# A new order of the four engines' calls in the first stage, and a chain of waits between the last 16 scatters

## Chip, cores and metric

The kernel runs on one core of one Trainium2 chip. The metric is the device time of one execution in microseconds (us), lower being better; a comparison goes by the median of several runs.

## The reference

Input `x` has 16 sequences of 256 tokens with 128 channels, 4096 tokens in all, in float32. Two blocks follow each other, each with a residual and a plain layer norm behind it. The first is an RWKV block: layer norms, a shift by one token, three 128x128 projections (key, value, receptance), a recurrence over time, an output projection, and then a channel mix with a hidden width of 512. The second is a mixture of experts with 12 experts, top 2, beside a shared expert.

```python
x = L0_attn_x
x = layernorm(x + attn(x))          # ln0, ln1, shift, k/v/r, wkv, Wo, ln2, channel mix
def ffn(x):
    ys = geglu(xf @ Ws1 + bs1) @ Ws2 + bs2            # shared expert, hidden 256
    logits = (xf @ Wr + br) / 1.5
    top_val, top_idx = top_k(logits, 2); w = softmax(top_val)
    yE[e] = geglu(xf @ We1[e] + be1[e]) @ We2[e] + be2[e]   # hidden 384
    return ys + sum_k w_k * yE[top_idx_k]
x = layernorm(x + ffn(x))
```

## The kernel before

**Two stages.** The 4096 tokens are 32 tiles of 128, and 4 tiles make a chunk of 512, so there are 8 chunks (0 to 7). The first stage takes every chunk through the RWKV block, the router and the shared expert. The second stage takes 75 tiles of 128 rows, sorted by expert, through their expert, and a last part adds everything up and norms it.

**Four engines, four lists written out by hand.** In the first stage each step is a small function that one engine calls with a chunk number, and every engine runs its own list of calls, strictly in that order: DVE at L690 to L709, ACT at L839 to L864, POOL at L943 to L956, PE at L1140 to L1162. Steps wait for one another through semaphores inside the functions. The order of a list decides what an engine does while something it will need later is not ready yet; a wait at the head of a list holds up all that is behind it.

**The steps that matter here.** DVE: `stats0` to `stats3` (L482 to L526, the statistics of the norms), `prepare` (L442, mixes the weights that `keys(0)` needs), `maximum`, `gaps`, `weigh_v`, `states`, `carried`, `one_over`, `output` (the recurrence), `mix`, `x3` (L596, end of the block's two residuals), `logits`, `chosen` (L337) and `placed` (L361, the row number to which each token's copy goes), `shared_act` (L622) and `shared_take` (L630), `find_tiles` and `tell_tiles` (L642, L672, the list of tiles, in two parts). ACT: `norm0` to `norm3`, `affine1`, `below`, `factors`, `by_channel` (L777), `shared_gelu` (L824), `place_pad` (L829, one small DMA each), `first_take`. POOL: `deviation` (L891, 1/sqrt of the variance), `weigh0`, `shift0`, `add_new`, `residual` and `scatter_rows` (L405). PE: `turn1` to `turn3` (transposes, L965 to L968), `keys`, `values`, `receptance`, `rwkv`, `hidden`, `mixed_channels` (L1055), `router` (L1026), `prefix`, `shared_gate` (L1094), `shared_up` (L1088), `shared_back` (L1100), `tell` (L1111), `first_turn`, `first_gates`.

**The scatters.** Each of the 32 tiles is written twice, once for each chosen expert, by an indirect DMA issued on POOL's queue (L413): 128 rows of 544 bytes go to places in DRAM by the indices of `placed`. That is 64 scatters. `placed(v, b)` frees 16 of them at a time (`slots_ready`). The first 48 count on the semaphore `dispatched`, the last 16 (`LATE` = 48) on `dispatched_late`. POOL does not wait for their landing.

**Who reads the scattered rows.** SP waits until the first 48 have landed and then loads rows for tiles 0 to 4 and onward (L1189), ten buffers deep. The first 35 tiles (`AHEAD`) need the first 48 scatters alone; only ahead of tile 35 does SP wait for the late 16. Behind its last scatter POOL's queue goes on with the second stage, where it issues one indirect DMA for each finished tile (L1235, 128 rows of 512 bytes to `routed_rows`) when DVE has written `yo` (L1288). There are ten `yo` buffers (`YO` = 10), so DVE waits ahead of tile n for the landing of tile n-10.

**The second stage's start.** PE needs both parts of the tile list (`bias_ready` at 2), seven of the eight `shared_take`, all `shared_gelu`, and the first rows and weights. Its last work of the first stage is `shared_up(7, 1)` and `shared_back(7)`; `tell(1)`, nine small products, makes the second part of the tile list.

## Time and profile before

| | us |
|---|---|
| median of 3 runs (461.55 to 463.85) | 462.53 |
| the profiled execution | 463.21 |
| its span in the profile | 461.4 |
| PE / DVE / ACT / POOL busy | 390.9 / 310.2 / 293.0 / 246.7 |

Times inside the profile count from the start of the span; some 1.8 us of the execution's own time lie around the span. PE is TensorE, PEld its weight loads, DVE VectorE, ACT ScalarE, POOL GpSimd, SP the queue that issues the plain DMAs. The first stage ends where the first matmul of L1396 starts. In the chain of work that ended last, "another core or an unknown queue" (also "remote") stands where a wait ended on a semaphore whose last update the profile cannot lay to an instruction that ended just then. There is one core here, so it is no other core: it is a signal that came long after the record of the instruction that gives it.

### The profile page before, as it was taken

The page shows a single profiled execution, that of the slowest core. Times are in us where ns is not written, and L with a number is a line of the kernel's source. Part 1 is how long each engine was busy: PE and PEld are TensorE (multiplying, and loading weights), DVE is VectorE, ACT ScalarE, POOL GpSimd, SP SyncE. Part 2 cuts the span into 40 slices and gives each one's busy share as a digit, 9 for nine tenths or more (in the row PEclk, how much of TensorE's full clock was granted, in tenths as well). Part 3 has the DMA queues.
Part 4 walks back from the last instruction along what each step waited for, and adds up shares of the span by engine and source line. Part 5 has one row for each costly group of instructions (what it writes and reads, how often), then busy time and mean ns, then how long its engine had stood idle before and what let it go on. Part 6 is the DMA issues. An engine that isn't in the chain of part 4 may idle for free.

```text
span 461.4 us, 9878 instructions
## 1 busy us (share of the span) xinstructions
PE 390.9 (85%) x2487; PEld 302.6 (66%) x2487; DVE 310.2 (67%) x1097; ACT 293.0 (64%) x723; POOL 246.7 (53%) x300
## 2 busy tenths in 40 slices
PE   0757799998988888976799499999999999999690
PEld 0224466757746565654344179999999999999530
DVE  6979988999996995741372266666666656665183
ACT  4478799989796955633121067777777766777062
POOL 4756855648388867777347114444444444444252
PEclk9978799999999999997899599999999999999997
DMA  8699100000003101011262137777776776762483
GB/s 230 151 288 348 46 0 1 1 1 1 2 18 104 32 13 44 30 50 42 82 203 83 54 136 248 259 244 261 247 254 243 258 250 238 253 239 104 132 328 106
DMA packets 47248, 64.86 MB, mean 141 GB/s; under 512 B 8797, under 2 KB 31069, under 8 KB 47193
## 3 DMA queue, kind: packets, MB, share of 16 engines
q1 hardware_dynamic: 42584, 54.50, 34.9%
q0 software_dynamic: 4448, 9.38, 6.1%
q8 instruction: 22, 0.36, 0.4%
q10 hardware_dynamic: 160, 0.35, 0.3%
q14 instruction: 34, 0.27, 0.2%
HBM read 21.65 MB, written 13.91 MB: 77 GB/s over the span
## 4 chain that ended last, share of the span: by engine, by line
PE 55%; DVE 14%; ACT 9%; another core or an unknown queue 8%; issue 5%; POOL 4%; DMA 2%; POOLq 0%; SPq 0%; DVEq 0%; ACTq 0%
PE bank L1396 22%; PE bank L1414 11%; DVE bst L487 3%; PE bank L1042 3%; ACT z L725 2%; PE bank L1060 2%; PE bank L1441 2%; PE bank L1108 2%; PE bank L1388 2%; DVE rec L576 1%; PE bank L1091 1%; DMA we_sb<-routed_rows 1%; PE bank L983 1%; PE bank L1071 1%
## 5 line engine op out<-in xcount | busy, mean ns | idle before, releaser
L1235 POOL DMA_INDIRECT routed_rows<-yo,goes_to x75 | 71.8, 957 | 103.8 <-DVE yo L1288 101.4
L1396 PE MATMUL bank<-xT,w 128*128 128x128 f32 x896 | 112.9, 275 | 0.0
L1396 PEld LDWEIGHTS bank<-xT,w 128*128 128x128 f32 x896 | 106.4, 192 | 0.8 <-issue 0.5
L1280 DVE SCALAR_TENSOR_TENSOR actT<-bank,tile_bias,gl 128x128 f32<-128x128 f32 x225 | 65.4, 346 | 24.8 <-ACT gl L1348 13.5
L413 POOL DMA_INDIRECT dispatched_rows<-rows_all,slot_i x64 | 64.3, 1005 | 30.1 <-issue 17.7
L1348 ACT ACTIVATE gl<-bank,tile_bias 128x128 f32<-128x128 f32 x225 | 66.2, 363 | 15.2 <-PE bank L1396 7.9
L1414 PE MATMUL bank<-we_sb,actT 128*128 x450 | 62.8, 276 | 1.0 <-DVE yo L1288 0.9
L1414 PEld LDWEIGHTS bank<-we_sb,actT 128*128 128x128 f32 x450 | 56.1, 192 | 1.5 <-issue 1.5
L1288 DVE SCALAR_TENSOR_TENSOR yo<-bank,goes,wb 128x128 f32<-128x128 f32 x75 | 26.3, 351 | 36.7 <-PE bank L1414 33.0
L1342 ACT ACTIVATE xT<-bank 128x128 f32<-128x128 f32 x74 | 20.5, 277 | 25.2 <-PE bank L1388 24.9
L1042 PE MATMUL bank<-xk,wfk_sb 128*128 128x512 f32 x64 | 33.0, 625 | 3.4 <-DVE xk L593 1.8
L1358 ACT ACTIVATE wb<-be_all,goes 128x128 f32 x75 | 30.1, 402 | 6.2 <-issue 5.5
L627 DVE SCALAR_TENSOR_TENSOR below_m<-bank,v_sb,below_p 128x512 f32<-128x512 f32 x16 | 11.8, 749 | 32.1 <-remote 24.4
L1060 PEld LDWEIGHTS bank<-wfv_sb,kf 128*128 128x128 f32 x256 | 29.4, 192 | 5.1 <-ACT kf L822 4.6
L983 PE MATMUL bank<-hT,mixa 128*128 128x512 f32 x48 | 27.0, 646 | 6.6 <-ACT hT L761 5.7
L1060 PE MATMUL bank<-wfv_sb,kf 128*128 128x128 f32 x256 | 30.4, 277 | 2.3 <-ACT kf L822 2.3
L827 ACT ACTIVATE below_p<-bank,v_sb 128x512 f32<-128x512 f32 x16 | 10.9, 684 | 31.1 <-PE bank L1097 17.8
L576 DVE RECIPROCAL rec<-nd 128x512 f32<-128x512 f32 x8 | 26.7, 3341 | 0.0
L984 PE MATMUL bank<-hT,mixb 128*128 128x512 f32 x48 | 26.0, 625 | 0.0
L1091 PE MATMUL bank<-xnT_all,ws_sb 128*128 128x512 f32 x32 | 18.9, 683 | 6.0 <-DVE below_m L627 6.0
L818 ACT ACTIVATE kf<-bank 128x512 f32<-128x512 f32 x32 | 18.6, 588 | 6.0 <-PE bank L1042 4.3
L1378 ACT ACTIVATE x_all<-bank,fnm,frs 128x128 f32<-128x128 f32 x28 | 10.5, 456 | 15.9 <-POOL fnm L1244 15.9
(220 smaller groups left out, 764.6 us busy)
## 6 DMA issues: line engine op xcount, KB each, us to landing
w<-we_sb SPq DMA_DIRECT2D x75, 384.0 KB
x_all<-dispatched_rows SPq DMA_DIRECT2D x75, 68.0 KB
we_sb<-we SPq DMA_DIRECT2D x1, 4608.0 KB
we_sb<-routed_rows SPq DMA_DIRECT2D x8, 512.0 KB, 7.4
rows_all<-x SPq DMA_DIRECT2D x8, 256.0 KB, 5.1
out<-x_all SPq DMA_DIRECT2D x8, 256.0 KB, 2.3
routed_rows<-yo,goes_to POOLq DMA_INDIRECT x75
dispatched_rows<-rows_all,slot_i POOLq DMA_INDIRECT x64
```

Of the source, the lines that this page charges most:

```text
L413: ng.indirect_dma_start(dispatch, bass.IndirectOffsetOnAxis(ap=slot_i[:, k, n:n + 1], axis=0), rows_all[:, n, :], None).then_inc(s["dispat ...
L576: nv.reciprocal(rec[:, :], nd[:, 1, :]).then_inc(s["rec_ready"], 1)
L983: nt.matmul(o, mixa[:, n, :], hT[:, :, 1:T + 1], start=True, stop=False)
L1042: nt.matmul(pf[j % 2][:, :], wfk_sb[:, j * P:(j + 1) * P], xk2[:, :], start=True, stop=True).then_inc(s["fk_ready"], 1)
L1060: last = nt.matmul(pkv[:, n * P:(n + 1) * P], kf[:, j, n * P:(n + 1) * P], wfv_sb[:, j, :], start=j == 0, stop=j == HF - 1)
L1235: ng.indirect_dma_start(routed, bass.IndirectOffsetOnAxis(ap=goes_to[n // U % DB][:, n % U:n % U + 1], axis=0), yo[n % YO][:, :], None).th ...
L1280: nv.scalar_tensor_tensor(actT[n % UA][:, at], ps_a[j][:, 0:P], tile_bias[:, j, n:n + 1], gl[n % 2][:, at], ALU.add, ALU.mult).then_inc(s2 ...
L1288: nv.scalar_tensor_tensor(yo[n % YO][:, :], ps_y[:, 0:C], goes[n // U % DB][:, n % U, 1:2], wb[n % 2][:, :], ALU.mult, ALU.add).then_inc(s ...
L1348: na.activation(gl[n % 2][:, j * P:(j + 1) * P], ps_g[j][:, 0:P], ACT.Gelu, bias=tile_bias[:, HK + j, n:n + 1]).then_inc(s2["gelu_ready"], 1)
L1358: na.activation(wb[n % 2][:, :], be2_all[:, ds(e * C, C)], ACT.Copy, scale=goes[n // U % DB][:, n % U, 1:2]).then_inc(s2["wb_ready"], 1)
L1396: return nt.matmul(to[:, 0:P], w1[m][:, off:off + P], xT[m][:, :], start=True, stop=True)
L1414: last = nt.matmul(ps_y[:, 0:C], actT[m][:, j * P:(j + 1) * P], we2_sb[:, ds(e, 1), j, :].rearrange("p a c -> p (a c)"), start=j == 0, sto ...
```

## The change

Two things. In `scatter_rows` each of the last 16 scatters but the first waits until the one ahead of it has landed (16 increments of `dispatched_late` for each). And the four lists of the first stage stand in another order. No step is added or left out, and every step is the same as before; the second stage is not touched. In the cut diff a line of "..." stands for lines of the lists that are left out.

```diff
@@ -410,6 +410,8 @@
                 for b, (lo, hi) in enumerate(BATCH):
                     if n == lo * CT and k == 0:
                         g.wait_ge(s["slots_ready"], b + 1)
+                if i > LATE:
+                    g.wait_ge(s["dispatched_late"], 16 * (i - LATE))
                 ng.indirect_dma_start(dispatch, bass.IndirectOffsetOnAxis(ap=slot_i[:, k, n:n + 1], axis=0), rows_all[:, n, :],
                                       None).then_inc(s["dispatched_late" if i >= LATE else "dispatched"], 16)
 
@@ -687,26 +689,27 @@
-            stats0(0); turn_rows(); stats0(1); first_rows(); stats1(0); prepare(); stats0(2); stats0(3); number_rows(); stats0(4); stats1(1); stats0(5); maximum(0); gaps(0)
-            stats0(6); stats1(2); weigh_v(0); states(0); carried(0); maximum(1); gaps(1); one_over(0); output(0)
...
-            stats2(7); chosen(v, 2); shared_act(0, 1); x3(6); mix(7); stats3(6)
-            shared_act(1, 0); placed(v, 2, pT[:, PT_PREFIX]); find_tiles(0); leave_tiles(); x3(7); shared_act(1, 1); stats3(7)
-            shared_take(0); logits(6); shared_act(2, 0); shared_act(2, 1); tell_tiles(0); logits(7); chosen(v, 3)
-            shared_take(1); shared_act(3, 0); shared_act(3, 1); placed(v, 3, pT[:, PT_PREFIX])
-            count_pads(); shared_act(4, 0); shared_act(4, 1); shared_take(2); shared_take(3); find_tiles(1); shared_act(5, 0)
-            shared_act(5, 1); shared_take(4); shared_act(6, 0); shared_act(6, 1); shared_take(5); tell_tiles(1)
-            shared_act(7, 0); shared_act(7, 1); shared_take(6); shared_take(7)
+            stats0(0); turn_rows(); stats0(1); first_rows(); stats1(0); stats0(2); stats0(3); prepare()
+            stats0(4); stats1(1); stats0(5); maximum(0); gaps(0); number_rows(); stats0(6); stats0(7); stats1(2)
...
+            stats2(7); placed(v, 1, pT[:, PT_PREFIX]); shared_act(1, 0); logits(5); chosen(v, 2); mix(7)
+            shared_take(0); shared_act(1, 1); x3(6); stats3(6); placed(v, 2, pT[:, PT_PREFIX]); find_tiles(0)
+            x3(7); stats3(7); shared_act(2, 0); shared_take(1); shared_act(2, 1); logits(6); shared_act(3, 0)
+            shared_act(3, 1); leave_tiles(); tell_tiles(0); logits(7); chosen(v, 3); shared_take(2)
+            shared_act(4, 0); shared_act(4, 1); placed(v, 3, pT[:, PT_PREFIX]); count_pads(); shared_take(3)
+            shared_take(4); shared_act(5, 0); shared_act(5, 1); find_tiles(1); shared_act(6, 0)
+            shared_act(6, 1); shared_take(5); shared_act(7, 0); shared_act(7, 1); tell_tiles(1); shared_take(6)
+            shared_take(7)
...
@@ -836,32 +839,32 @@
-            norm0(0); decays(); norm0(1); norm1(0); affine1(0); norm0(2); norm1(1); below(0); factors(0); gate(0)
-            affine1(1); norm0(3); norm1(2); below(1); factors(1); norm0(4); affine1(2); gate(1); x1(0); norm1(3)
...
-            relu(7, 1); square(7, 1); relu(7, 2); square(7, 2); relu(7, 3); square(7, 3); norm3(6)
-            shared_gelu(1, 1); gate2(7); by_channel(6); shared_gelu(2, 0); shared_gelu(2, 1)
-            norm3(7); by_channel(7); shared_gelu(3, 0); shared_gelu(3, 1); fallen(a, 3)
-            shared_gelu(4, 0); shared_gelu(4, 1); place_pad(7); shared_gelu(5, 0); place_pad(8)
-            shared_gelu(5, 1); place_pad(9); shared_gelu(6, 0); place_pad(10); shared_gelu(6, 1); place_pad(11)
-            shared_gelu(7, 0); first_take(0); shared_gelu(7, 1)
+            norm0(0); norm0(1); norm1(0); decays(); affine1(0); norm0(2); norm0(3); norm1(1); below(0)
+            factors(0); affine1(1); norm1(2); norm0(4); gate(0); below(1); norm0(5); factors(1); x1(0); gate(1)
...
+            square(7, 3); norm3(6); shared_gelu(2, 0); gate2(7); shared_gelu(2, 1); shared_gelu(3, 0); norm3(7)
+            by_channel(6); shared_gelu(3, 1); by_channel(7); shared_gelu(4, 0); fallen(a, 3); shared_gelu(4, 1)
+            shared_gelu(5, 0); shared_gelu(5, 1); shared_gelu(6, 0); place_pad(7); shared_gelu(6, 1)
+            place_pad(8); place_pad(9); shared_gelu(7, 0); shared_gelu(7, 1); place_pad(10); place_pad(11)
+            first_take(0)
...
@@ -940,20 +943,17 @@
-            deviation0(0); deviation0(1); deviation(0, "1"); weigh0(1)
-            shift0(1); deviation0(2); deviation(1, "1"); weigh0(2); shift0(2)
-            deviation(2, "1"); deviation0(3); add_new(0); weigh0(3); shift0(3); weigh0(4); deviation(3, "1")
-            deviation(0, "2"); add_new(1); deviation0(4); shift0(4); residual(0); weigh0(5)
-            deviation(4, "1"); deviation(1, "2"); shift0(5); add_new(2); deviation(0, "3"); residual(1)
-            deviation(5, "1"); deviation(2, "2"); add_new(3); residual(2); deviation(1, "3")
-            weigh0(6); shift0(6); deviation(3, "2"); add_new(4); weigh0(7); deviation(6, "1")
-            shift0(7); deviation(2, "3"); deviation(7, "1"); residual(3); deviation(4, "2"); add_new(5)
-            residual(4); deviation(3, "3"); scatter_rows(g, 0, 7); deviation(5, "2"); scatter_rows(g, 7, 9)
-            add_new(6); scatter_rows(g, 9, 11); deviation(4, "3"); scatter_rows(g, 11, 13); residual(5)
-            scatter_rows(g, 13, 15); deviation(6, "2"); scatter_rows(g, 15, 16); add_new(7); deviation(5, "3")
-            residual(6); scatter_rows(g, 16, 23); deviation(7, "2"); scatter_rows(g, 23, 28); residual(7)
-            scatter_rows(g, 28, 29); deviation(6, "3"); scatter_rows(g, 29, 38); deviation(7, "3")
-            scatter_rows(g, 38, SLOTS // P)
+            deviation0(0); deviation0(1); deviation(0, "1"); deviation0(2); weigh0(1); shift0(1); weigh0(2)
+            deviation(1, "1"); shift0(2); deviation0(3); weigh0(3); shift0(3); deviation0(4); deviation(2, "1")
+            add_new(0); weigh0(4); shift0(4); weigh0(5); shift0(5); deviation(3, "1"); deviation(0, "2")
+            add_new(1); deviation(4, "1"); weigh0(6); residual(0); add_new(2); deviation(1, "2"); residual(1)
+            deviation(0, "3"); shift0(6); deviation(5, "1"); deviation(2, "2"); add_new(3); weigh0(7); shift0(7)
+            residual(2); deviation(1, "3"); deviation(3, "2"); deviation(6, "1"); add_new(4); residual(3)
+            deviation(2, "3"); deviation(7, "1"); deviation(4, "2"); add_new(5); residual(4); deviation(3, "3")
+            deviation(5, "2"); add_new(6); scatter_rows(g, 0, 7); residual(5); deviation(4, "3")
+            scatter_rows(g, 7, 9); add_new(7); deviation(6, "2"); scatter_rows(g, 9, 16); residual(6)
+            deviation(5, "3"); deviation(7, "2"); scatter_rows(g, 16, 23); residual(7); deviation(6, "3")
+            scatter_rows(g, 23, 29); deviation(7, "3"); scatter_rows(g, 29, SLOTS // P)
...
@@ -1137,29 +1137,30 @@
-            turn1(0); keys(0); values(0); receptance(0); turn1(1); keys(1); turn1(2); receptance(1); values(1)
-            rwkv(0); values(2); keys(2); turn2(0); receptance2(0); hidden(0, 0); turn1(3); receptance(2)
...
-            shared_up(1, 1); turn3(6); shared_gate(2, 0); router(6); shared_gate(2, 1); shared_up(2, 0); tell(0)
-            shared_gate(3, 0); shared_back(1); turn3(7); shared_up(2, 1); router(7); shared_up(3, 0)
-            shared_gate(3, 1); shared_back(2); shared_up(3, 1); prefix(3); shared_gate(4, 0); shared_back(3)
-            shared_up(4, 0); shared_gate(4, 1); shared_up(4, 1); shared_gate(5, 0); shared_back(4)
-            shared_gate(5, 1); shared_up(5, 0); shared_up(5, 1); shared_gate(6, 0); shared_gate(6, 1)
-            shared_back(5); shared_up(6, 0); shared_gate(7, 0); shared_up(6, 1); tell(1); shared_gate(7, 1)
-            shared_up(7, 0); shared_back(6); first_turn(0); shared_up(7, 1); first_turn(1); first_gates(); shared_back(7)
+            turn1(0); keys(0); values(0); turn1(1); receptance(0); keys(1); receptance(1); values(1); rwkv(0)
+            turn1(2); keys(2); turn2(0); values(2); receptance2(0); turn1(3); hidden(0, 0); hidden(0, 1)
...
+            hidden(7, 3); prefix(2); receptance2(7); mixed_channels(7); shared_back(1); shared_gate(2, 1)
+            shared_gate(3, 0); shared_up(2, 1); shared_up(3, 0); turn3(6); shared_back(2); shared_up(3, 1)
+            shared_gate(3, 1); router(6); tell(0); turn3(7); shared_gate(4, 0); router(7); shared_back(3)
+            shared_gate(4, 1); shared_gate(5, 0); shared_up(4, 0); shared_up(4, 1); prefix(3); shared_up(5, 0)
+            shared_back(4); shared_gate(5, 1); shared_up(5, 1); shared_gate(6, 0); shared_up(6, 0)
+            shared_up(6, 1); shared_gate(6, 1); shared_back(5); shared_gate(7, 0); shared_gate(7, 1)
+            shared_back(6); shared_up(7, 0); shared_up(7, 1); tell(1); first_turn(0); shared_back(7)
+            first_turn(1); first_gates()
```

In the part of the lists that is cut out the calls are shifted against one another by a few places: on DVE `number_rows`, `stats0(7)` and the later `stats1` calls, on PE `rwkv` earlier against `hidden`, on ACT `norm0` and `norm1` earlier against `relu` and `square`.

## Rows read from the trace of the kernel before

**Rows 1.** The page: chain of work that ended last, by engine

```profile
PE 55%; DVE 14%; ACT 9%; another core or an unknown queue 8%; issue 5%; POOL 4%; DMA 2%; POOLq 0%; SPq 0%; DVEq 0%; ACTq 0%
```

**Rows 2.** The chain in order of time, 200 to 260: start, us, what

```profile
200.83 10.34 another core or an unknown queue
...
217.94 7.77 another core or an unknown queue
...
246.67 12.49 another core or an unknown queue
```

**Rows 3.** Timeline of PE, 203 to 269: start, us, engine, line, operation [idle before]

```profile
203.25 0.60 PE L967 MATMUL bank<-ident,rows_all 128*128 128x128 f32 x4
...
248.50 1.02 PE L1091 MATMUL bank<-xnT_all,ws_sb 128*128 128x512 f32 x2
...
251.64 1.51 PE L1121 MATMUL bank<-of_expert,be_sb 12*128 12x40 f32 x12
253.07 1.12 PE L1097 MATMUL bank<-xnT_all,ws_sb 128*128 128x512 f32 x2
260.18 2.04 PE L1091 MATMUL bank<-xnT_all,ws_sb 128*128 128x512 f32 x2 [5.98 <-DVE below_m L627]
262.01 3.20 PE L1108 MATMUL bank<-below_m,ws_sb 128*128 128x512 f32 x4
...
267.12 1.98 PE L1108 MATMUL bank<-below_m,ws_sb 128*128 128x512 f32 x4
268.95 1.05 PE L1396 MATMUL bank<-xT,w 128*128 128x128 f32 x8
```

**Rows 4.** Timelines of ACT and DVE: what ended the two longest of those waits

```profile
211.19 0.60 ACT L779 ACTIVATE xnT_all<-bank 128x512 f32<-128x512 f32 x1 [10.36 <-remote]
```

```profile
259.28 1.41 DVE L627 SCALAR_TENSOR_TENSOR below_m<-bank,v_sb,below_p 128x512 f32<-128x512 f32 x2 [12.61 <-remote]
```

**Rows 5.** Timeline of POOL: scatters 29, 38, 47, 48, 63, then the second stage's

```profile
198.26 1.03 POOL L413 DMA_INDIRECT dispatched_rows<-rows_all,slot_i  x1 [0.16 <-issue]
...
211.33 1.03 POOL L413 DMA_INDIRECT dispatched_rows<-rows_all,slot_i  x1 [0.16 <-issue]
...
222.77 0.96 POOL L413 DMA_INDIRECT dispatched_rows<-rows_all,slot_i  x1 [0.31 <-issue]
236.08 0.96 POOL L413 DMA_INDIRECT dispatched_rows<-rows_all,slot_i  x1 [12.36 <-DVE slot_i L383]
...
255.01 0.95 POOL L413 DMA_INDIRECT dispatched_rows<-rows_all,slot_i  x1 [0.31 <-issue]
273.55 0.96 POOL L1235 DMA_INDIRECT routed_rows<-yo,goes_to  x1 [17.59 <-DVE yo L1288]
275.67 0.96 POOL L1235 DMA_INDIRECT routed_rows<-yo,goes_to  x1 [1.16 <-DVE yo L1288]
```

**Rows 6.** Busy time by stretch: start:end, length, PE, PEld, DVE, ACT, POOL, PEclk, DMA, GB/s

```profile
60.00:200.00 140.00, 128.74 (x736) 89.57 (x735) 120.33 (x344) 115.94 (x224) 93.56 (x115) 1.00 0.07 22
...
204.70:211.90 7.20, 0.01 (x1) 0.00 (x1) 3.84 (x13) 0.60 (x1) 5.94 (x9) 0.87 0.14 48
...
246.70:259.20 12.50, 7.50 (x31) 3.79 (x29) 0.00 (x0) 0.80 (x2) 7.13 (x8) 0.81 0.21 67
259.20:269.00 9.80, 8.67 (x19) 3.92 (x20) 5.46 (x14) 2.44 (x6) 0.00 (x0) 0.72 0.16 43
269.00:300.00 31.00, 31.00 (x275) 30.65 (x274) 19.77 (x73) 22.12 (x73) 12.44 (x13) 1.00 0.67 235
```

**Rows 7.** The chain at the end: the last tile's indirect DMA, issue to landing

```profile
430.62 2.50 DMA routed_rows<-yo,goes_to
```

**Rows 8.** Timelines of DVE and PE at the start

```profile
14.18 0.87 DVE L487 BATCH_NORM_STATS2 bst<-rows_all 128x6 f32<-128x128 f32 x4
...
16.55 0.16 DVE L468 CAST x_all<-pad_i 128x23 f32<-128x23 int32 x1
```

```profile
15.56 2.07 PE L983 MATMUL bank<-hT,mixa 128*128 128x512 f32 x2 [0.66 <-ACT hT L755]
```

More of the change, by code:

```diff
@@ new lines, in attention_scalar @@
+            affine2k(1); norm0(7); gate2(1); x1(2); norm3(0); relu(1, 0); square(1, 0); gate(3); by_channel(0)
+            relu(1, 1); relu(1, 2); affine1(4); square(1, 1); square(1, 2); norm2(2); relu(1, 3); square(1, 3)
+            norm1(5); affine2(2); affine2k(2); below(4); factors(4); gate2(2); x1(3); norm3(1); gate(4)
+            affine1(5); relu(2, 0); relu(2, 1); norm2(3); relu(2, 2); relu(2, 3); by_channel(1); square(2, 3)
+            square(2, 1); square(2, 0); square(2, 2); norm1(6); affine2k(3); affine2(3); below(5); factors(5)
@@ new lines, in attention_scalar @@
+            relu(3, 0); x1(4); square(3, 0); relu(3, 1); gate2(3); norm3(2); relu(3, 2); affine1(6)
+            square(3, 2); relu(3, 3); norm2(4); by_channel(2); square(3, 1); square(3, 3); norm1(7)
+            fallen(a, 0); affine2k(4); affine2(4); gate(5); below(6); gate2(4); factors(6); x1(5); norm3(3)
+            relu(4, 0); by_channel(3); relu(4, 1); gate(6); affine1(7); norm2(5); relu(4, 2); relu(4, 3)
+            square(4, 2); square(4, 0); square(4, 1); square(4, 3); affine2(5); below(7); factors(7)
@@ new lines, in attention_tensor @@
+            turn2(3); values(5); mixed_channels(2); router(1); rwkv(4); hidden(3, 0); hidden(3, 1)
+            receptance2(3); turn1(6); hidden(3, 2); receptance(5); hidden(3, 3); turn3(2); keys(6); values(6)
+            turn2(4); mixed_channels(3); receptance2(4); rwkv(5); router(2); receptance(6); hidden(4, 0)
+            hidden(4, 1); turn3(3); hidden(4, 2); turn1(7); hidden(4, 3); prefix(0); keys(7); turn2(5)
+            values(7); mixed_channels(4); receptance2(5); rwkv(6); shared_gate(0, 0); router(3); hidden(5, 0)
@@ new lines, in attention_tensor @@
+            hidden(5, 1); shared_up(0, 0); hidden(5, 2); hidden(5, 3); shared_gate(0, 1); shared_up(0, 1)
+            turn3(4); receptance(7); mixed_channels(5); turn2(6); rwkv(7); receptance2(6); router(4)
+            hidden(6, 0); hidden(6, 1); shared_gate(1, 0); hidden(6, 2); prefix(1); shared_back(0); hidden(6, 3)
+            turn3(5); shared_up(1, 0); shared_gate(1, 1); router(5); shared_up(1, 1); turn2(7)
+            shared_gate(2, 0); mixed_channels(6); hidden(7, 0); hidden(7, 1); shared_up(2, 0); hidden(7, 2)
```

67 lines of the change are left out of this document (24 added, 43 removed).

## The prediction

> **What bounds the kernel now.** I read the chain of work that ended last first. PE has 55% of it, and 8% stands as "another core or an unknown queue" [rows 1]. On one core that can only be a signal that came late. In order of time, three pieces make 30.6 us of it: 10.3, 7.8 and 12.5 us, all between 200 and 260 [rows 2]. So the end of the first stage, not its middle, holds the largest loss that is nobody's work.
>
> Next I asked what the late signals have in common. PE's four transposes of chunk 6 are recorded at 203.25 and take 0.6 us, yet ACT, which waits for them, starts at 211.19 [rows 3, 4]. The `shared_up(6, 0)` of 248.50 is done at 249.5, and the DVE instruction that reads it starts at 259.28 [rows 3, 4]. In both cases the signal that is late is PE's. PE then has nothing to do: 0.01 us busy of 7.2 in the stretch from 204.7 [rows 6]. POOL's timeline fits: these stretches are the ones in which POOL issues scatters back to back. Scatters 29 to 47 run from 198.26 to 222.77, with one norm step among them ahead of 38, and 48 to 63 from 236.08 to 255.01, one each 1.26 us (18.93 / 15) [rows 5]. Between the two bursts no such piece stands in the chain. The waits end soon after a burst does: 225.7 against the last issue at 222.77, 259.2 against 255.01 [rows 2, 5]. An indirect DMA on this queue needs 2.50 us from issue to landing [rows 7], so at a spacing of 1.26 two are always in flight. In the second stage they come 2.12 us apart [rows 5], and there PE is busy 31.0 of 31.0 us [rows 6]. My reading: scatters closer together than they land hold up PE's signals. It is an inference from when things happen; no row shows the path.
>
> From 60 to 200 the stage is another thing: PE is busy 128.7 of 140 us and DVE 120.3 [rows 6]. An order can win there only what PE idles, 11.3 us.
>
> **The change, part by part.** The sum goes against the profiled execution, 463.2 us (span 461.4 and 1.8 around it), which lies 0.7 above the median of 462.5.
>
> *The waits between the late scatters.* Each now costs POOL the landing, 2.50 us [rows 7], and the 0.3 us of issue that stands between two scatters already [rows 5]. The spacing grows from 1.26 to 2.8. From the first late scatter at 236.1 the last is issued at 236.1 + 15 x 2.8 = 278.1 instead of 255.0, and POOL is free at 279.1. Behind the waiting scatters on POOL's queue stands only the second stage: its first indirect DMA, now at 273.55 [rows 5]. SP needs the late rows ahead of tile 35, some 50 us after the second stage starts even with ten buffers of lead, so that wait hides. The direct cost is zero as long as ten `yo` buffers cover the delay: if the second stage starts 8 us earlier (below), the first `yo` is there at 265.3, and (279.1 - 265.3) / 2.12 = 6.5 tiles queue up, under ten. Without that cover, each tile over ten would cost 2.1 us.
>
> *What the waits free.* If one scatter in flight leaves PE's signals alone, the 12.5 us go. PE ran ahead in part: 7.5 us of work in the 12.5 [rows 6], up to 254.2 (253.07 + 1.12). From there it would go on at once. What it still did in the trace, from 260.18 to 268.95, is 8.77 us. Two pieces of it ran at the lower of the two clocks after PE's idle time: 2.04 against 1.02 for L1091 and 3.20 against 1.98 for L1108 [rows 3]; the granted clock of the stretch is 0.72, a mix of 2.4 and 1.2 GHz [rows 6]. Without the idle time these 2.2 us go too. So L1396 starts at 254.2 + 6.5 = 260.7 in place of 268.95: -8.2. The new list sets `tell(1)` behind `shared_up(7, 1)`; its twelve small products take 1.5 us [rows 3], and DVE's copies that all of the second stage waits for then run beside `shared_back(7)`. That is the same PE work at a worse place; I take 0.2 of loss, at most 1. Term: **-8**, bounds 0 (nothing is freed) and -12.5.
>
> *Scatters 29 to 47 behind the norm of chunk 7.* In the trace nine of them precede that norm's 1/sqrt; scatter 38 behind it starts at 211.33 [rows 5]. In the new list all 19 are behind it. So chunk 7's last norm, transpose and router should pass before the burst, where now ACT waits for chunk 6's transpose until 211.19 and for chunk 7's until 225.7 [rows 2, 4]. ACT's list also takes `norm3(7)` ahead of `by_channel(6)`, and PE gets five more shared products ahead of `turn3(6)`. Against that the burst starts later: at some 209 I would say, so its last scatter is issued at 209 + 18 x 1.26 = 231.7, 9 us later than 222.77, without a pause. The router's work no longer sits in it, but the shared expert's does, and the late 16 follow soon. SP's tile loads need the landing, 234.2; they then take a few us and the second stage needs them only at 260. Bounds: -11 (the 10.3 and most of what PE loses with it go) and +8.5 (the same stall, ending that much later). PE does some work even in a stall (7.5 of 12.5 [rows 6]), so I stay near the middle: **-2**.
>
> *The start.* `prepare()` moves behind `stats0(2)` and `stats0(3)`, which take 14.18 to 16.55 [rows 8]. The mixed weights, ready just ahead of 14.18, are then ready 2.4 later, at 16.5, and `keys(0)`, which starts at 15.56, starts 1 us later. In return the norm of chunks 2 and 3, and so `x0` of chunk 1, come up to 3 us earlier, and `number_rows` (1.2 us) leaves DVE's way to `maximum(0)`. **-1**, bounds -2 and +1.
>
> *The middle.* `rwkv`, `norm0`, `norm1`, `add_new` and the statistics shift by a few places. POOL now does `deviation(5, "2")` and `add_new(6)`, for which others wait, ahead of its first scatter; no step is added. With PE 92% busy I take **0**, bounds -4 and +5 (a misplaced call holds the recurrence of one chunk).
>
> Sum: 463.2 - 8 - 2 - 1 = **452.2**, say 452.
>
> **A rule against it.** The rows above tie PE's late signals to DMAs. The Trainium skill, "SBUF — State Buffer", section "SBUF: two separate sides", says that "A DMA cannot be slowed by a compute op, and vice versa". By that rule the scatters are innocent, the waits free nothing, and only the order works. This is the first rival below.
>
> **The rivals.**
>
> *The stall stays.* The late signals come from something else in these stretches (SP's pads and ACT's pads are issued there too), or four in a row suffice with any spacing. For it: the trace has stretches with scatters and no late signal, such as 236 to 246. Against it: all three long pieces lie in or just behind a burst. Then 463.2 - 1 - 2 = 460.2, with the new place of the burst uncertain; say 460.5.
>
> *The stall moves into the second stage: slower.* When POOL comes free at 279.1 it has 6.5 tiles to catch up, at 1.26 us each against 2.12 a tile: 13.8 / 0.86 = 16 indirect DMAs back to back. That is the same burst as the 16 late scatters, which cost 12.5 us, now in a stage where PE has no idle time at all [rows 6]. Price up to 12.5: 452.2 + 12.5 = 464.7, and about 465 to 469 when the first burst also ends later. It decides from a backlog of some three tiles on (seven in a row), that is, from a late chain that ends 6 us behind the first `yo`. For it: the arithmetic. Against it: these rows are 512 bytes, not 544, and the signals there have a tile of slack only in part.
>
> *Both stalls go.* Chunk 7 passes before the burst and the shared work no longer waits for PE's signals: -11 in place of -2, which gives 443 to 444.
>
> **How the numbers follow.** Forecast 0.52, stall stays 0.17, moved into the second stage 0.17, both go 0.14. A run of this kernel tells 0.5%, 2.3 us, from no change. Faster by more than that (under 460.2): the forecast and the last rival, less a little, with a few hundredths of the first, 0.67. Within: most of the first, 0.16. Slower: 0.17. The range takes in the last rival at its low end and the first at its high end: 444 to 462; only the slower rival and some tail are left out.
>
> **What would show it.** Right: late scatters 2.5 to 3 us apart; no "unknown" piece of over 3 us while they run; PE at its upper clock in the last 10 us of the first stage; L1396 first at 255 to 260; POOL's first L1235 some 13 us behind its `yo`. Wrong: the piece of 12 us still there with the late scatters 2.8 apart (the rule above holds); PE with idle time between 275 and 300 (moved); a piece of over 15 us at 210 to 235 (the burst). If the stage reaches 200 more than 3 us off, the middle was mispriced.

## The result, and the profile after

The changed kernel took **473.7 us** (472.8 to 474.7, 4 runs) beside 463.2 us for the kernel before on the same chip (461.6 to 464.1, 4 runs): ratio 1.0246, 95% interval 1.0204 to 1.0288. Forecast were 452 and a range of 444 to 462. The change is slower, and the forecast had the wrong sign.

| | before | after |
|---|---|---|
| profiled execution, span | 463.2, 461.4 | 472.8, 471.0 |
| first gate products of the experts (L1396, now L1397) | 268.95 | 259.92 |
| from there to the end | 192.5 | 211.1 |
| first / last late scatter | 236.08 / 255.01 | 240.16 / 285.22 |
| POOL's first indirect DMA of the second stage | 273.55 | 286.48 |

So the first stage is 9.0 us shorter, where 11 were forecast, and the second 18.6 longer, where 0 was forecast. The page of after, part 4 (the chain that ended last, by engine), against [rows 1]:

```profile
PE 47%; DVE 12%; DMA 11%; POOL 8%; issue 8%; ACT 6%; another core or an unknown queue 5%; POOLq 0%; DVEq 0%; ACTq 0%; SPq 0%
```

DMA has 11% of the chain where it had 2%; 9% are landings of POOL's scatters, by the same part of the page. The unknown part fell from 8% to 5% only. The chain's longest pieces from 200 us on say where (start, us, what), against [rows 2]:

```profile
212.95 6.01 another core or an unknown queue
220.49 12.12 another core or an unknown queue
...
258.55 2.26 DMA dispatched_rows<-rows_all,slot_i
261.08 3.39 DMA dispatched_rows<-rows_all,slot_i
264.74 4.11 DMA dispatched_rows<-rows_all,slot_i
269.12 3.30 DMA dispatched_rows<-rows_all,slot_i
...
282.05 2.91 DMA dispatched_rows<-rows_all,slot_i
285.22 0.96 POOL dispatched_rows L415
```

Two things are to be seen. The 18.1 us in the first burst (two pieces) are as long as before (10.3 and 7.8), and the piece of 12.5 us ahead of the second stage is gone. But the late chain, which the waits turn into landing after landing, runs on until POOL starts on the second stage's DMAs. Its landings take 2.3 to 2.5 us until 260; behind that, with SP loading a tile every 2.12 us beside them, they take 2.3 to 4.1. What follows, on DVE and PE, against [rows 5, 6]; first the timeline of DVE (start, us, engine, line, operation, count, idle time before and who ended it):

```profile
289.31 0.35 DVE L1289 SCALAR_TENSOR_TENSOR yo<-bank,goes,wb 128x128 f32<-128x128 f32 x1 [5.04 <-DMA routed_rows<-yo,goes_to]
289.58 0.86 DVE L1281 SCALAR_TENSOR_TENSOR actT<-bank,tile_bias,gl 128x128 f32<-128x128 f32 x3
...
297.27 0.35 DVE L1281 SCALAR_TENSOR_TENSOR actT<-bank,tile_bias,gl 128x128 f32<-128x128 f32 x1 [4.96 <-remote]
```

Then PE's:

```profile
290.11 1.65 PE L1415 MATMUL bank<-we_sb,actT 128*128 x6 [4.07 <-DVE yo L1289]
...
295.56 0.49 PE L1397 MATMUL bank<-xT,w 128*128 128x128 f32 x2 [0.46 <-ACT gl L1349]
297.67 0.49 PE L1397 MATMUL bank<-xT,w 128*128 128x128 f32 x2 [1.62 <-issue]
299.80 0.54 PE L1397 MATMUL bank<-xT,w 128*128 128x128 f32 x2 [1.64 <-DVE actT L1281]
```

And busy time by stretch (stretch, length, then busy us of PE, PEld, DVE, ACT, POOL; granted clock; DMA share; GB/s):

```profile
60.00:200.00 140.00, 134.27 (x769) 93.44 (x769) 120.94 (x341) 115.85 (x223) 86.41 (x107) 1.00 0.06 20
...
280.00:290.00 10.00, 6.04 (x55) 5.80 (x53) 3.41 (x14) 4.60 (x16) 4.79 (x5) 0.99 0.66 228
290.00:300.00 10.00, 6.17 (x34) 5.61 (x35) 1.56 (x6) 1.48 (x4) 7.59 (x8) 0.84 0.17 54
300.00:320.00 20.00, 16.89 (x118) 16.19 (x118) 9.26 (x34) 11.02 (x35) 7.14 (x9) 0.74 0.48 167
```

This is one chain of events with two losses. All ten `yo` buffers are full, so DVE waits 5.04 us for the first landing (its releaser is the DMA). Then POOL sends twelve DMAs 1.26 us apart (286.48 to 300.37), and in that burst PE gets on by two products every 2.1 us, where the twelve of a tile otherwise take 1.5; DVE's wait of 4.96 us ends by a signal of PE's that is late (`remote`). The clock falls to a mix of its two levels (0.74 from 300 to 320) and the pace of 2.12 us a tile is back only at 311. The sign that the prediction had named for a moved stall, PE with idle time between 275 and 300, is there: 12.2 us busy of the 20 from 280 on.

### The profile page after: what moved, and what is told of

Read it like the earlier page. It is cut to its first block, busy times and chain, and to the rows that moved or that the text cites. A ratio compares the mean times of both kernels' runs of the same rounds, so it can differ in the third digit from the quotient of the medians.

```text
span 471.0 us, 9878 instructions
## 1 busy us (share of the span) xinstructions
PE 395.1 (84%) x2487; PEld 305.5 (65%) x2487; DVE 309.7 (66%) x1097; ACT 292.2 (62%) x723; POOL 245.8 (52%) x300
## 4 chain that ended last, share of the span: by engine, by line
PE 47%; DVE 12%; DMA 11%; POOL 8%; issue 8%; ACT 6%; another core or an unknown queue 5%; POOLq 0%; DVEq 0%; ACTq 0%; SPq 0%
PE bank L1397 19%; PE bank L1415 10%; DMA dispatched_rows<-rows_all,slot_i 9%; PE bank L1442 3%; PE bank L1060 3%; PE bank L1042 2%; ACT z L728 2%; PE bank L983 2%; PE bank L984 2%; DVE rec L578 1%; DVE bst L489 1%; PE bank L1389 1%; POOL rstd L915 1%; POOL rstd L903 1%
## 5 line engine op out<-in xcount | busy, mean ns | idle before, releaser
L1397 PE MATMUL bank<-xT,w 128*128 128x128 f32 x896 | 116.3, 280 | 5.8 <-DVE actT L1281 3.2
L1397 PEld LDWEIGHTS bank<-xT,w 128*128 128x128 f32 x896 | 109.1, 196 | 6.9 <-DVE actT L1281 3.7
L415 POOL DMA_INDIRECT dispatched_rows<-rows_all,slot_i x64 | 62.9, 982 | 56.3 <-DMA dispatched_rows<-rows_all,slot_i 30.7
L1415 PE MATMUL bank<-we_sb,actT 128*128 x450 | 65.0, 282 | 6.6 <-DVE yo L1289 5.0
L1415 PEld LDWEIGHTS bank<-we_sb,actT 128*128 128x128 f32 x450 | 58.0, 197 | 7.6 <-issue 7.6
L983 PE MATMUL bank<-hT,mixa 128*128 128x512 f32 x48 | 28.5, 678 | 11.0 <-ACT th L810 5.7
L1042 PE MATMUL bank<-xk,wfk_sb 128*128 128x512 f32 x64 | 32.0, 605 | 2.3 <-ACT kf L821 2.3
L984 PE MATMUL bank<-hT,mixb 128*128 128x512 f32 x48 | 27.2, 651 | 0.0
L830 ACT ACTIVATE below_p<-bank,v_sb 128x512 f32<-128x512 f32 x16 | 10.8, 682 | 22.8 <-PE bank L1097 16.1
L944 POOL TENSOR_TENSOR s<-x1c,rows_all 128x512 f32<-128x512 f32 x8 | 10.5, 1318 | 27.4 <-DVE x3c L607 27.0
L983 PEld LDWEIGHTS bank<-hT,mixa 128*128 128x128 f32 x48 | 8.8, 213 | 20.6 <-issue 12.2
```

The source lines that it names most:

```text
L415: ng.indirect_dma_start(dispatch, bass.IndirectOffsetOnAxis(ap=slot_i[:, k, n:n + 1], axis=0), rows_all[:, n, :], None).then_inc(s["dispat ...
L983: nt.matmul(o, mixa[:, n, :], hT[:, :, 1:T + 1], start=True, stop=False)
L984: nt.matmul(o, mixb[:, n, :], hT[:, :, 0:T], start=False, stop=True).then_inc(s[name], 1)
L1042: nt.matmul(pf[j % 2][:, :], wfk_sb[:, j * P:(j + 1) * P], xk2[:, :], start=True, stop=True).then_inc(s["fk_ready"], 1)
L1397: return nt.matmul(to[:, 0:P], w1[m][:, off:off + P], xT[m][:, :], start=True, stop=True)
L1415: last = nt.matmul(ps_y[:, 0:C], actT[m][:, j * P:(j + 1) * P], we2_sb[:, ds(e, 1), j, :].rearrange("p a c -> p (a c)"), start=j == 0, sto ...
```

## The experiments

Every experiment was timed beside the kernel before, in the same session on the same chip. One thing has to be told first, as it orders all that follows: **the sessions were of two kinds**. In three of them, that of the result among them, the kernel before took 463.0 to 463.8 us. In four it took 438.3 to 440.4, on four chips, and one of these was met in both kinds. I call the first kind sessions with late signals, and each trace shows by itself which kind it is from: in the eleven traces from sessions without them no wait at all is put down to `remote`, in the nine others 7 to 17 waits are, the longest of them 5.6 to 19.3 us. Otherwise the traces of one program differ little: that of the kernel before stays within 2.3 us of its counterpart (the kernel with a held DMA, further down, which is the same up to there) until 185 us and starts the second stage 22.7 behind it.

| | sessions without late signals | with |
|---|---|---|
| the kernel before | 438.3 to 440.4 us | 463.0 to 463.8 us |
| new order alone | 0.983, 0.982, 0.986 | 1.015, 1.019 (each with one more small edit) |
| waits alone, old order | 1.001 | 1.011 |
| **both: the change** | **1.013, 1.012** | **1.025** |
| waits in pairs | 0.983 | |
| the change with 14 `yo` buffers | | 1.016 |
| new order, nine more scatters ahead of chunk 7's norm | | 1.017 |
| the kernel before with a held DMA | 1.000 | |
| paced, scatter 48 on (1.8 us apart) | | 0.995 |
| paced, scatter 29 on (1.8 us), pads spread, 14 buffers | 1.003 | 0.972 |
| the same with 1.38 us for 29 to 47 | 0.986, 0.989 | |

(Ratios to the kernel before of the same session, as they are on record; the intervals are in the text, 0.003 to 0.008 to either side. A ratio need not be the quotient of the two medians beside it. For two kernels it matters: with 14 buffers the medians give 1.024, with nine scatters ahead 1.009. The kernel before took 455.4 to 465.3 us in that session.)

**The order alone** (session without late signals).

```diff
-                if i > LATE:
-                    g.wait_ge(s["dispatched_late"], 16 * (i - LATE))
```

> The changed kernel without the waits: the new order alone. Theory A (the order is worth little, the waits win in the first stage and lose more in the second): the 16 late scatters run 1.26 us apart from about 240 to 259, a piece of about 12 us stands there again, L1395 (gate products of the experts) starts at 266 to 270 where it starts at 259.9 with the waits, POOL never queues more than one tile in the second stage, which then takes 192 us as before. Time 459 to 464. Rival B (the order is what costs): 470 or more, with the first burst of scatters, 29 to 47, as the place. Rival C (the second stage is slow for something else than the late chain, such as the weights' or rows' loads): second stage of over 200 us without the waits too, 469 or more.

432.4 us beside 439.2, ratio 0.983 [0.979, 0.986]: a gain that no theory had. Scatters 29 to 63 run in one burst of 35 (200.8 to 243.9, 1.27 apart), and the piece of 12 us that theory A expects of it is not there: no part of the chain is unknown. L1395 starts at 235.5.

```profile
PE 62%; DVE 11%; POOL 9%; issue 6%; ACT 6%; DMA 2%; POOLq 0%; DVEq 0%; ACTq 0%; SPq 0%
```

So here a burst held up nothing, and the order's own worth can be read. Busy time of PE, the kernel before (with its held DMA of tile 30, further down) and then the new order:

```profile
60.00:200.00 140.00, 129.70 (x736) 0.99 0.07 22
```

```profile
60.00:200.00 140.00, 136.66 (x776) 1.00 0.06 21
```

PE gets 7.0 us more done in the middle, for which I had taken 0. By 246.3 and 235.5 for the first gate products the whole first stage gives 10.8 (9.4 and 7.3 in the two repeats further down); the time falls by 5.3 to 8.5 us in the three.

**The waits alone** (same session), and later in one with late signals.

```diff
+                if i > LATE:
+                    g.wait_ge(s["dispatched_late"], 16 * (i - LATE))
```

> The kernel before with the waits alone, in the old order. Theory A: L1398 or so starts 6 to 9 us earlier than the 268.95 of before, the late chain lasts 45 us from 236 to 281, POOL is 6 to 8 tiles behind when it starts on the second stage's DMAs and sends 12 to 16 of them back to back; PE stalls there. With less backlog than in the changed kernel (its chain starts 4 us earlier) the loss is 10 to 18: 464 to 473. Rival B (the order is what costs): the waits alone give the 8 us and lose nothing, 453 to 457. Rival C: second stage 192 us whatever the late chain does.

439.7 beside 439.2, ratio 1.001 [0.998, 1.004]: nothing gained, nothing lost. Gate products from 245.2, POOL free at 265.5, first `yo` at 249.2: 7.7 tiles of backlog, under ten. The 19 DMAs back to back that follow cost nothing here.

> The kernel before with the waits alone once more, for the case that this is a chip with late signals (before at 463; then all of this holds): second stage begins 6 to 9 us earlier than 268.95, the late chain ends at about 281, some 7 tiles of backlog, 14 to 18 DMAs back to back in the second stage and a stall of 8 to 14 there: 463 to 470, ratio 1.00 to 1.015. Beside a kernel before of 439 it repeats 1.001.

467.2 beside 463.8, ratio 1.011 [1.004, 1.017]. Gate products from 260.7, which is 8.2 us ahead of the 268.95 of [rows 3], and the second stage takes 206.0. The backlog was 7.4 tiles (280.4 less 264.7, by 2.12), no buffer was short, and still 13 us went. DVE's longest wait in the burst and the chain:

```profile
287.38 0.35 DVE L1290 SCALAR_TENSOR_TENSOR yo<-bank,goes,wb 128x128 f32<-128x128 f32 x1 [5.78 <-remote]
```

```profile
282.33 7.77 issue
290.12 2.76 another core or an unknown queue
293.33 2.79 PE bank L1398 x10
```

The catch-up burst runs from 280.4 on. That is the burst's stall by itself, without the wait for a buffer.

**A burst put into the kernel before** (session without).

```diff
-                g.wait_ge(s2["yo_ready"], n + 1)
+                g.wait_ge(s2["yo_ready"], n + 1 if n != 30 else n + 8)
```

> The kernel before, with one edit in the second stage alone: POOL's DMA of tile 30 waits until DVE has given tile 37, so that eight are queued and then go back to back, as after the late chain, but with no scatter of the first stage, no full set of the ten buffers and 50 us later. Theory A (DMAs back to back hold up PE's signals, wherever they are): some 18 in a row at 1.26 us, PE in stalls of 5 to 12 us with the lower clock after it: 470 to 476. Rival C (the second stage's loss comes from waiting for one of the ten buffers, or from the late scatters): 463 to 464.5, no stall.

439.8, ratio 1.000 [0.997, 1.002], 18 DMAs 1.26 us apart from 329.5 on and PE busy 80.0 of 80 us from 320 to 400. Theory A's forecast fell. As the session then proved to be of the other kind, it shows only that a burst is harmless there.

**Waits in pairs** (same session).

```diff
-                if i > LATE:
+                if i > LATE and (i - LATE) % 2 == 0:
```

> The changed kernel, but only every second late scatter waits (for all ahead of it): pairs 1.26 us apart, then one landing. Chain of 8 x (1.3 + 2.7) = 32 us, from 240 to 272, where it was 45. Theory A: two in a row do not hold up a signal for long, the first stage ends as with all the waits (L1397 at 260 to 262), the backlog is (272 + 1 - 263.5) / 2.12 = 4 to 5 tiles, no wait for a yo buffer, some 9 to 11 DMAs back to back, whose stall costs 3 to 7: 456 to 464. Rival (two in flight are enough to hold signals up): the 12 us piece is back and the second stage begins at 266 or later: 464 to 468.

432.9, ratio 0.983 [0.979, 0.986], as the order alone: the chain ends at 254.9, (256.2 - 242.6) / 2.12 = 6.4 tiles queue, no buffer is short.

**The changed kernel again** (session without, and once more in the last one).

> The changed kernel itself, with no edit, because in the four runs so far the kernel before took 439.2 us instead of 463.2 and no signal of PE was late in any of the four, bursts or not. If the late signals belong to the chip or the session and not to the kernel: beside a kernel before of 439 the changed kernel takes 432 to 434 (as the order alone), since a catch-up of 12 DMAs back to back then costs nothing, plus up to 4 for the wait for one of the ten buffers, so 432 to 438, ratio 0.985 to 0.998. If the kernel before is at 463 again, the changed kernel is at 474, and the late signals are back in both. Rival (the full chain of waits costs 9 us on any chip): 440 to 446 beside 439.

> The changed kernel on the same chip: 1.02 to 1.03 with late signals, 1.013 without.

444.6 beside 440.0, ratio 1.013 [1.009, 1.017], and 443.9 beside 438.3, 1.012 [1.005, 1.018]. The rival was right: the full chain of waits costs time in the new order without a late signal too, 11 to 12 us against the order alone (10.9 where both ran in one session). In the old order it cost nothing there (1.001). One row of DVE's timeline holds most of it:

```profile
262.49 0.35 DVE L1289 SCALAR_TENSOR_TENSOR yo<-bank,goes,wb 128x128 f32<-128x128 f32 x1 [0.46 <-issue]
263.29 0.87 DVE L1281 SCALAR_TENSOR_TENSOR actT<-bank,tile_bias,gl 128x128 f32<-128x128 f32 x3 [0.45 <-PE bank L1397]
273.70 0.35 DVE L1289 SCALAR_TENSOR_TENSOR yo<-bank,goes,wb 128x128 f32<-128x128 f32 x1 [9.54 <-DMA routed_rows<-yo,goes_to]
```

The gate products start at 235.1, the chain of landings lasts until 270.2 all the same, and (271.5 - 238.6) / 2.12 = 15.5 tiles should queue where ten have room. PE then stands, and runs at the lower clock for a while:

```profile
260.00:280.00 20.00, 11.39 (x86) 11.16 (x85) 5.68 (x21) 6.98 (x23) 10.61 (x12) 0.74 0.38 135
```

**Fourteen buffers, pads spread, prepare() back, nine scatters ahead** (one session, with late signals). The last three of these are without the waits.

```diff
-    XB, YO = 2 * U, 2 * U
+    XB, YO = 2 * U, 14
```

> The changed kernel with all its waits, with 14 yo buffers in place of ten (the final loads take the semaphores of the first loads, nothing else changes). Theory A (the waits lose their time on a chip without late signals because DVE waits for one of the ten buffers, 9.1 of 11.2 us idle from 262.5 to 273.7): the late chain still ends at 270, tile 14 is due at 270 to 271, so at most 2 us of wait are left: 434 to 437 beside 439.5, ratio 0.988 to 0.995 against 1.013. Rival (the loss comes from the 20 DMAs back to back or from late rows): stays within 2 us of 444.6.

474.1 beside 463.0, ratio 1.016 [1.009, 1.023]. The wait for a buffer is gone and the time is not:

```profile
292.18 0.35 DVE L1289 SCALAR_TENSOR_TENSOR yo<-bank,goes,wb 128x128 f32<-128x128 f32 x1 [0.46 <-issue]
...
302.47 0.35 DVE L1289 SCALAR_TENSOR_TENSOR yo<-bank,goes,wb 128x128 f32<-128x128 f32 x1 [5.20 <-remote]
...
311.53 0.35 DVE L1281 SCALAR_TENSOR_TENSOR actT<-bank,tile_bias,gl 128x128 f32<-128x128 f32 x1 [8.22 <-remote]
```

While fourteen DMAs go back to back (292.3 to 308.7), two tiles pass from 292.2 to 312.8 where ten would. More room made the backlog and so the burst longer. (My figures were for the other kind of session, so the buffers' 9.5 us there were not tried.)

```diff
-                if n == 2 * U:
-                    for pad in range(SP_PADS):
-                        place_pad(pad)
                 if n >= 2 * U:
                     load_weights(n - U, owners.pop(n - U))
+                if n >= 2 * U and n % 2 == 0 and (n - 2 * U) // 2 < SP_PADS:
+                    place_pad((n - 2 * U) // 2)
```

> The new order without the waits, and SP's seven pad copies, which run in one block of 8.4 us (235.8 to 244.4) ahead of the weights of tile 5, spread: one behind every second tile's loads from the tenth on. The theory: with a first stage that is 10.8 us shorter the block of pads is what PE waits for (2.6 us idle ahead of the gate products at 247.76, and 3.1 us more for the second stage than before). Expected: that gap gone, second stage 192.5 to 193.5 us in place of 196.0, ratio 0.975 to 0.978 where the order alone has 0.983 (some 429.5 beside 439.5). Rival (the gap comes from the rows of tile 5, behind scatter 47): unchanged, 0.983. If the chip is one with late signals (before at 463), no figure.

470.5, ratio 1.015 [1.011, 1.020]. No figure was given for this kind of session, and the pads' question stays open: in the two later runs of the order alone, with the gate products at 236.9 and 239.0, the second stage took 193.1 and 192.1 with the pads in one block.

```diff
-            stats0(0); turn_rows(); stats0(1); first_rows(); stats1(0); stats0(2); stats0(3); prepare()
+            stats0(0); turn_rows(); stats0(1); first_rows(); stats1(0); prepare(); stats0(2); stats0(3)
```

> The new order without the waits, with prepare() put back ahead of stats0(2) and stats0(3). The prediction gave the start 1 us of gain from the new place; by that this one takes 1 us longer than the order alone, ratio 0.985. Rival 1 (the new place costs, since the first mixed products start 0.3 to 2.8 us later up to chunk 1): 1 to 2 us shorter, 0.979 to 0.981. Rival 2 (the slack of the later chunks takes up either): 0.983, with L1395 first at 235 to 236.

471.2, ratio 1.019 [1.014, 1.024]. With `prepare()` back, DVE is 3.3 us later than in its neighbour with the pads spread at some 180 us, but the gate products start within 0.6 us of each other, 275.5 and 276.1: the late signals take what the start gives.

These two are the order without the waits in a session with late signals. Both start the second stage 6.5 to 7.1 us **later** than the kernel before. The longest pieces of their chains show where, of the kernel with the pads spread first:

```profile
198.64 5.40 another core or an unknown queue
...
216.56 19.28 another core or an unknown queue
```

Those of the other, `prepare()` back, are 4.59 and 13.48. The pieces of the first burst alone are 18 to 19 us, as much as both of [rows 2] together. Behind 250 us stand a further 13.4 us in the one and 10.9 in the other, about the 12.5 of [rows 2]. So the pieces are about as long as in the kernel before, but the first burst ends later (scatter 47 at 231.7 and 234.9 for 222.77). The next experiment puts the pause of the old order back into it.

```diff
-            scatter_rows(g, 23, 29); deviation(7, "3"); scatter_rows(g, 29, SLOTS // P)
+            scatter_rows(g, 23, 38); deviation(7, "3"); scatter_rows(g, 38, SLOTS // P)
```

> The new order without the waits, but nine more scatters (29 to 37) go ahead of the norm of chunk 7, as in the old order. That norm comes 9 x 1.26 = 11.3 us later on POOL. The prediction gave 2 us to having it ahead. By it: L1395 first at 237 to 238, 434 to 435, ratio 0.987. Rival (chunk 7's router has slack because the shared expert's products fill PE): within 0.5 of the order alone, 0.983. Rival (it is on the path in full, through the last slots, tell(1) and the tiles): 241 or later, 438 and more.

467.1, ratio 1.017 [1.010, 1.023], gate products at 272.3 where the two above have 275.5 and 276.1. By the traces and by the medians (467.1 for 470.5 and 471.2) nine scatters ahead of the norm of chunk 7 are 3 to 4 us better here, not worse. The recorded ratios, 1.017 beside 1.015 and 1.019, don't show it, so I hold it for likely and not for shown.

**POOL paced, no waits for landings** (session with late signals). A 1/sqrt of one column (0.57 us) behind each late scatter and each of the second stage's first 60 DMAs puts them 1.81 us apart.

```diff
+                if i >= LATE:
+                    ng.tensor_tensor(spent[:, i - 29:i - 28], eps4[:, 0:1], half[:, 0:1], ALU.pow)
...
+                if n < 60:
+                    ng.tensor_tensor(spent[:, 35 + n:36 + n], eps4[:, 0:1], half[:, 0:1], ALU.pow)
```

> The new order, the landing waits replaced by a small 1/sqrt of POOL behind each of the 16 late scatters and behind each of the second stage's first 60 indirect DMAs, so that two of them are never less than about 2.0 us apart from scatter 48 on; nothing waits for a landing. Late chain 32 us in place of 45. On a chip with late signals (before at 463): the piece of 12 us ahead of the second stage is gone as with the waits, the second stage begins at 260 to 263, POOL is 4 to 5 tiles behind, never fills the ten buffers and never runs at 1.26 us, so the second stage takes 193 to 196: 455 to 459, ratio 0.98 to 0.99, where order alone has 1.015 to 1.019 and order with waits 1.025. Rival (2.0 us apart holds signals up too): 465 or more. On a chip without late signals (before at 439): as the order alone, 432 to 434.

461.7 beside 463.8, ratio 0.995 [0.990, 1.000], the profiled execution 459.7. Gate products at 263.4 and a second stage of 194.5: as the waits in the first stage, and almost none of their 18.6 in the second. PE, 280 to 300 and 300 to 320:

```profile
280.00:300.00 20.00, 20.00 (x182) 1.00 0.74 255
300.00:320.00 20.00, 20.00 (x176) 1.00 0.75 254
```

> As the last, and the same pace from scatter 29 on, with SP's pad copies spread over the tiles and 14 yo buffers, so that no burst is left in the kernel at all. On a chip with late signals: both stalls of the first stage go, the second stage begins at 248 to 252, bound by SP's first tile loads behind scatter 47 (landed at 245), and the backlog of 10 to 11 tiles stays under 14: 445 to 450, ratio 0.96 to 0.975. If it stays over 458, the first stall is not the burst's. On a chip without late signals: first tiles' rows land 13 us later than in the order alone (247 in place of 229 to 237), so slower than it by 8 to 12: 440 to 444.

Here scatters 29 to 47 have the pace too, 1.83 us; 449.9 beside 463.8, ratio **0.972** [0.964, 0.980]. The stall behind scatter 29 is gone as well; all engines from 220 to 230 in the last kernel and then in this one:

```profile
220.00:230.00 10.00, 0.00 (x0) 0.00 (x0) 1.27 (x8) 0.00 (x0) 7.56 (x9) 0.62 0.26 92
```

```profile
220.00:230.00 10.00, 10.00 (x43) 5.32 (x43) 8.57 (x43) 2.76 (x5) 8.89 (x11) 1.00 0.62 232
```

It is the pace that does it: in the kernel with the pads spread and in the one with 14 buffers, both without a pace, PE was busy 0.00 us of these ten as well. What is left of late signals are short waits (5.6 us at most, behind the scatters up to 28, which have no pace, and one of 2.1 us at 278), and what bounds the start of the second stage is now the landing of scatter 47:

```profile
243.64 2.34 DMA dispatched_rows<-rows_all,slot_i
246.54 1.74 DMA x_all<-dispatched_rows
248.98 3.41 PE bank L1109 x4
254.63 1.34 PE bank L1399 x12
```

The second stage takes 198.5 there, more than the 194.5 with the late pace alone; that was not followed up.

The last two sessions were meant to be ones with late signals and were of the other kind.

> The version without bursts once more. On a chip with late signals it repeats 0.964 to 0.980. On one without (before at 439): the first tiles' rows come 10 us later than the order alone has them, second stage at 245 to 249, 440 to 444, ratio 1.00 to 1.01.

1.003 [1.000, 1.006], gate products at 243.0: where no signal is late, pacing the first burst gives the order's gain away.

> The new order without the waits once more. On a chip with late signals (before at 463): as the two kernels that differ from it by one small edit, second stage from 274 to 276, 468 to 471, ratio 1.012 to 1.02; so the order costs 6 to 8 there and the waits another 3 to 4, net of 12 to 15 gained in the first stage. Rival (the pads' edit or prepare() made those slow): 0.98 to 1.00. On a chip without late signals it repeats 0.983.

> On a chip with late signals (before at 463): second stage from 274 to 276, 468 to 471, ratio 1.012 to 1.02. Rival: 0.98 to 1.00. On one without: 0.982 again.

0.982 [0.977, 0.986] and 0.986 [0.981, 0.992].

> As the version without bursts (0.972 on a chip with late signals), but scatters 29 to 47 have only a small add of POOL between them: some 1.4 to 1.5 us apart in place of 1.83. The 48th lands 7 us earlier, at 239, and SP's first tile loads with it. If 1.45 is wide enough: second stage at 247 to 249 in place of 253.25, 445 to 447, ratio 0.962 to 0.968. If it is not: the idle time of PE at 218 to 235 is back in part, 452 or more, ratio over 0.975. On a chip without late signals: 0.985 to 0.995.

> On a chip with late signals: 0.962 to 0.968 if 1.45 us between scatters is wide enough, over 0.975 if not. On one without: 0.986 again.

0.986 [0.981, 0.990] and 0.989 [0.983, 0.995]. Scatters 29 to 47 were in fact 1.38 us apart. Whether that is wide enough where signals are late was not measured, so no one version is shown to be best in both kinds of session.

## Why the prediction was wrong

By its own steps:

- **The reading of the trace** (signals of PE held up by scatters closer than they land) held for the kind of session it was made in. Pacing the late scatters at 1.81 us removes the 12 us piece, pacing the rest removes the other stall, a catch-up of the second stage's DMAs brings it back there. The trace held a further case that the text didn't use: a piece of 4.2 us at 179.0, in a row of seven scatters (174.7 to 182.3). By what path a burst holds a signal up stays open. What it missed is that it is a state: in the other kind of session 35 scatters in a row (200.8 to 243.9) went with no late signal. A trace shows which kind it is from, but not that there is another. The rival that the scatters are innocent named a rule of the Trainium skill, "SBUF — State Buffer", section "SBUF: two separate sides"; the paced kernels speak against that rival in one kind of session, and nothing does in the other. They don't test the sentence itself: what came late were signals between engines, and the sentence is of compute ops and DMAs slowing each other.
- **The waits' direct cost, 0: the step that failed.** "6.5 tiles queue up, under ten" was (279.1 - 265.3) / 2.12. Measured is (286.5 - 263.4) / 2.12 = 10.9. The 9.3 us between them ((10.9 - 6.5) x 2.12) are: the chain starts 4.1 later (240.16 for 236.08), because the slots of the last batch are ready later; it lasts 45.1 us where 42 were counted, its steps (landing and issue) being 2.62 us up to 261 and 3.45 behind it, beside the tile loads, where the text had 2.8 for all; the first `yo` is 1.9 earlier; and 0.3. The price named for the uncovered case, 2.1 us a tile, was too small by far, since it left out what the backlog does when it is worked off. In place of 0 the second stage lost 18.6 us: 5.0 of waiting for a buffer, and about the 13.5 that the waits cost in the old order with no buffer short (206.0 for 192.5).
- **The stall moved into the second stage** was the slower rival, with chance 0.17 and a price up to 12.5. Place and mechanism are right: it is shown alone by the waits in the old order, and it is gone when the DMAs are paced (194.5). The text had worked out 16 DMAs in a row, as many as the burst that it priced at 12.5; the evidence for this rival was as good as for the gain, and its chance should have been.
- **What the waits free, -8**: right in the old order (260.7, so -8.2), too small in the new one: 263.3 with the waits (and 14 buffers) beside 275.5 and 276.1 without, in one session, is 12 to 13.
- **Scatters 29 to 47 behind the norm, -2**: likely the wrong sign where signals are late. Nine of them ahead are worth 3 to 4 us by traces and medians; the bound of +8.5 had priced just that, a burst that ends later. Without late signals it was not tried.
- **The start, -1**: right in sign, 3.3 us at 180 us, 0.6 the other way at the end of the stage.
- **The middle, 0, bounds -4 and +5**: out of bounds, if PE's busy time is the measure. It is busy 7.0 us more between 60 and 200 without late signals and 5.5 more with them ([rows 6] against the row above). Which of the moves does it was not tried.

The sum for the session of the result: the order alone was not run there itself, but with one small edit it stands at 1.015 and 1.019, some 7 to 9 us. So the terms of the order, -3 in the sum, miss by 10 to 12 there, as much as those of the waits. Of the order's cost the place of the nine scatters explains 3 to 4; the rest stays open. The waits add about 3: they give 12 to 13 in the first stage and cost 15 to 19 in the second. Without late signals it is the reverse: the order gives 5 to 8 us, and the waits, which have nothing to free, take 11 to 12.

## What to carry to other kernels

A wait for landing is a throttle whose rate depends on the other traffic and which nothing lets up: count when the chain *ends*, at the landing time beside the loads of the next stage, and what then stands in the queue. A backlog that fits its buffers is not free either, if it is worked off in a burst; a fixed small gap between the DMAs (0.57 us of dummy work here) took the burst away in both stages, where the wait only moved it. The gap is worth that only where signals are late; elsewhere it used up what the order had given (1.003 for 0.983). And a stall that may be a state of the session has to be looked for in more than one session before a change is built on it.

## What was not expected of the hardware

The late signals come and go between sessions, on one and the same chip (463.0 and 440.4 us for the same kernel), and are 22.7 us of the kernel before by the start of the second stage (268.95 and 246.3). With them, indirect DMAs in a row, 1.26 us apart, go with late signals of PE: six or seven in a row with a wait of up to 5.6 us, 16 to 19 in a row with up to 19.3 in one piece, and at 1.8 us from one to the next one of 2.1 us is the longest. Without them, 35 in a row hold up nothing. Landing of one scatter with none beside it was 2.3 to 2.5 us in the result's trace, and 2.3 to 4.1 beside the tile loads; without late signals up to 5.4. What makes a session the one or the other stays open.
